# The new state of a recurrence made on VectorE ahead of the last tanh, instead of inside it

## The reference

```python
x = x + _L1_ffn_ref(_layernorm(x, axis=-1)[None], U_i, V_i, b_i, ...)[0]

def step(carry, xs):
    h, c = carry
    xi_t, xf_t, xg_t, xo_t = xs
    i_t = jax.nn.sigmoid(xi_t + h @ V_i)
    g_t = jnp.tanh(xg_t + h @ V_c)
    o_t = jax.nn.sigmoid(xo_t + h @ V_o)
    c_new = h * c + i_t * g_t
    h_new = o_t * jnp.tanh(c_new)
    return ((h_new, c_new), h_new)
```

## Time and profile before

| | |
|---|---|
| runs, us | 3303.53, 3307.72, 3311.19 |
| median, us | 3307.72 |
| span of the profiled execution, us | 3296.9 |
| TensorE busy with matmuls | 1510.9 us, 46% |
| VectorE busy | 1953.7 us, 59%, 13086 instructions |
| ScalarE busy | 1441.9 us, 44%, 8446 instructions |
| granted TensorE clock in the recurrence | 0.5 of full speed (1.2 GHz) |

### The profile page before, as it was taken

How to read it: one execution, slowest core, us unless ns; L and a number is a source line. 1 busy time by engine, 2 the same in 40 slices (tenths; PEclk the granted TensorE clock), 3 DMA queues, 4 the chain that set the end, 5 groups by cost and what they waited for, 6 DMA issues and landing times.

```text
span 3296.9 us, 86333 instructions
## 1 busy us (share of the span) xinstructions
PE 1510.9 (46%) x26414; PEld 1141.6 (35%) x26414; DVE 1953.7 (59%) x13086; ACT 1441.9 (44%) x8446; POOL 169.9 (5%) x130
## 2 busy tenths in 40 slices
PE   4989575434343434333443434343434343434343
PEld 4444323333333333333333333333333333333333
DVE  5557896555555555555555555555555555555555
ACT  5331134444444444444444444444444444444444
POOL 0620271000000000000000000000000000000000
PEclk8999885555555555555555555555555555555555
DMA  6010000000000000000000000000000000000000
GB/s 225 1 32 0 0 5 1 2 3 2 3 2 3 2 3 2 3 2 3 2 2 3 2 3 2 3 2 3 2 3 2 3 2 3 2 2 2 3 2 15
DMA packets 13012, 29.04 MB, mean 9 GB/s; under 512 B 1971, under 2 KB 9654, under 8 KB 10422
## 3 DMA queue, kind: packets, MB, share of 16 engines
q1 hardware_dynamic: 10406, 22.02, 1.9%
q10 hardware_dynamic: 2064, 0.55, 0.1%
HBM read 21.52 MB, written 1.05 MB: 7 GB/s over the span
## 4 chain that ended last, share of the span: by engine, by line
ACT 37%; PE 37%; DVE 15%; issue 9%; DMA 1%; SPq 0%; DVEq 0%; POOL 0%; ACTq 0%; POOLq 0%
PE psum L490 21%; ACT work L663 18%; ACT work L659 11%; DVE work L984 11%; ACT work L655 8%; PE psum L412 4%; PE psum L494 3%; PE psum L353 2%; PE psum L474 2%; PE psum L473 2%; PE psum L364 1%; DVE work L898 1%; DVE FT L935 1%; DMA work<-in_adj_dram 1%; PE psum L392 0%
## 5 line engine op out<-in xcount | busy, mean ns | idle before, releaser
L490 PE MATMUL psum<-work,MASK 128*128 128x1 f16 x18432 | 951.5, 168 | 1656.3 <-DVE work L984 1582.5
L490 PEld LDWEIGHTS psum<-work,MASK 128*128 128x128 bf16 x18432 | 802.7, 107 | 1817.5 <-DVE work L984 1741.0
L655 ACT ACTIVATE work<-psum 128x1 f32<-128x1 f32 x2048 | 351.2, 172 | 1471.0 <-PE psum L494 1471.0
L979 DVE TENSOR_SCALAR work<-work 128x1 f32<-128x1 f32 x2048 | 314.6, 154 | 732.1 <-ACT work L659 732.1
L663 ACT ACTIVATE work<-psum,work 128x1 f32<-128x1 f32 x2048 | 720.2, 352 | 0.0
L494 PE MATMUL psum<-work,MASK 128*128 128x1 f16 x6144 | 575.5, 168 | 0.0
L984 DVE CUSTOM_DVE_ANT_0 work<-work 128x1 f16<-128x1 f32 x2048 | 331.5, 162 | 295.3
L494 PEld LDWEIGHTS psum<-work,MASK 128*128 128x128 f16 x6144 | 432.3, 107 | 0.0
L990 DVE SCALAR_TENSOR_TENSOR work<-psum,work 128x1 f32<-128x1 f32 x2048 | 430.7, 210 | 0.0
L659 ACT ACTIVATE work<-psum 128x1 f32<-128x1 f32 x2048 | 414.9, 203 | 20.8 <-PE psum L494 20.8
L987 DVE TENSOR_TENSOR work<-work 128x1 f16<-128x1 f32 x2048 | 332.3, 162 | 72.1
(11 more groups left out here) (132 smaller groups left out, 1005.2 us busy)
## 6 DMA issues: line engine op xcount, KB each, us to landing
work<-in_adj_dram SPq DMA_DIRECT2D x16, 1024.0 KB, 5.3
work<-in_L_ffn_Wd_dram SPq DMA_DIRECT2D x4, 512.0 KB, 6.0
out_dram<-work SPq DMA_DIRECT2D x4, 256.0 KB, 2.4
work<-in_L_ffn_bd_dram SPq DMA_DIRECT2D x1, 512.0 KB, 6.8
W<-in_L_ffn_W_dram ACTq DMA_DIRECT2D x1, 256.0 KB, 2.8
watt<-in_L_gnn_w_att_dram ACTq DMA_DIRECT2D x2, 64.0 KB, 7.2
work<-in_L_gnn_Wq_dram SPq DMA_DIRECT2D x1, 64.0 KB, 8.1
Wfc<-in_L_gnn_W_fc_dram ACTq DMA_DIRECT2D x1, 64.0 KB, 5.8
```

The source lines that it names most:

```text
L490: nc.tensor.matmul(bank(NGATE * k + gate)[:, col:col + 1], Vparts[:, gate, part, :], h1[:, q:q + 1], start=False, stop=False, skip_group_c ...
L655: nc.scalar.activation(sig_i[:, q], bank(NGATE * k)[:, col:col + 1], ACT.Sigmoid).then_inc(i_ready, 1)
L979: v.tensor_scalar(o_scaled[:, q], sig_o[:, q], SCALE_H, None, ALU.mult).then_inc(o_scaled_ready, 1)
```

## The change

The tanh of g goes to a new SBUF column g_ in place of PSUM. VectorE waits for hc, sig_i and g at the head of its step and writes g * i + hc into PSUM bank 6 or 7. The last tanh waits for that alone (c_ready) and reads it, with no scale and no bias. Behind the product, VectorE does not make the state again; hc is made from the PSUM column, and the two waits there go.

```diff
-        c_, hc, tanh_c, sig_i, sig_o, o_scaled = (region(SMALL + 2 * k, 2) for k in range(6))
+        g_, hc, tanh_c, sig_i, sig_o, o_scaled = (region(SMALL + 2 * k, 2) for k in range(6))
...
-                    nc.scalar.activation(bank(6 + u % 2)[:, 0:1], bank(NGATE * k + 1)[:, col:col + 1], ACT.Tanh).then_inc(g_ready, 1)
+                    nc.scalar.activation(g_[:, q], bank(NGATE * k + 1)[:, col:col + 1], ACT.Tanh).then_inc(g_ready, 1)
...
-                    act.wait_ge(g_ready, t + 1)
-                    act.wait_ge(hc_ready, t + 1)
-                    nc.scalar.activation(tanh_c[:, q], bank(6 + u % 2)[:, 0:1], ACT.Tanh,
-                                         bias=hc[:, q], scale=sig_i[:, q]).then_inc(tanh_ready, 1)
+                    act.wait_ge(c_ready, t + 1)
+                    nc.scalar.activation(tanh_c[:, q], bank(6 + u % 2)[:, 0:1], ACT.Tanh).then_inc(tanh_ready, 1)
...
+                    dve.wait_ge(hc_ready, t + 1)
+                    dve.wait_ge(i_ready, t + 1)
+                    dve.wait_ge(g_ready, t + 1)
+                    v.scalar_tensor_tensor(bank(6 + u % 2)[:, 0:1], g_[:, q], sig_i[:, q], hc[:, q],
+                                           ALU.mult, ALU.add).then_inc(c_ready, 1)
                     dve.wait_ge(o_ready, t + 1)
                     v.tensor_scalar(o_scaled[:, q], sig_o[:, q], SCALE_H, None, ALU.mult).then_inc(o_scaled_ready, 1)
...
-                    dve.wait_ge(hc_ready, t + 1)
-                    v.scalar_tensor_tensor(c_[:, q], bank(6 + u % 2)[:, 0:1], sig_i[:, q], hc[:, q],
-                                           ALU.mult, ALU.add).then_inc(c_ready, 1)
-                    dve.wait_ge(c_ready, t + 1)
-                    v.scalar_tensor_tensor(hc[:, r], ring_h[:, u:u + 1], 1.0 / SCALE_H, c_[:, q],
+                    v.scalar_tensor_tensor(hc[:, r], ring_h[:, u:u + 1], 1.0 / SCALE_H, bank(6 + u % 2)[:, 0:1],
                                            ALU.mult, ALU.mult).then_inc(hc_ready, 1)
```

## The result

| | us |
|---|---|
| before, median (lowest to highest) | 3305.72 (3303.53 to 3311.19) |
| changed, median (lowest to highest) | 3669.31 (3666.64 to 3672.69) |
| ratio, 95% interval | 1.1101 (1.1085 to 1.1116) |
| span of the profiled execution, before and changed | 3296.9 and 3671.0 |

The change made the kernel 364 us slower. The forecast was 3577 with a range of 3480 to 3690; of the rivals, "the handoff or the write is dearer" stood at 3662 and 3686.

The account below looks back on a forecast made before the run. The prediction took the ring's latency per step as the bound: the path from the i gate to the product grows from 0.65 to 0.789 us, +0.139 in 1937 steps, 269 us, giving 3577 us; range 3480 to 3690.

Parts of the forecast that it names:

- the handoff or the write is dearer: Rival: g's handoff to VectorE takes 0.144 us (3662), or the state's PSUM write its upper bound (3686); chance 0.15.
- The path that sets the end: Latency once around the engines' ring of waits sets the time; TensorE's wait for the product grows some 265 us.
- The tie ahead of the product: Before, the tanh's path and the output gate's scaling path both reach VectorE's product at 0.65 us, within 0.01.
- The tanh at 0.172: ScalarE's last tanh, without its two operand columns, falls from 0.352 to 0.172 us, saving 0.180.
- The handoff from g to the state: From g's end on ScalarE to VectorE's state, behind a wait standing in front: 0.10 us.
- The state at 0.210: VectorE's new instruction making the state into PSUM lasts 0.210 us, like line 990 with the same operands.
- The handoff back and the last 0.03: From the state's end to ScalarE's tanh 0.035 us, and from the tanh's end to VectorE's product 0.03.
- How many steps pay: Of 2048 steps, 96 gate-input steps and 15 with TensorE stopped cover the added time; 1937 pay, 269 us.
- The scaling path at 0.02 under the tanh: VectorE's output gate scaling, now behind the state, lets the product start at 0.77 us, against 0.789 by the tanh.
- The rival that the wait in front costs no more than a carried one: Rival: g's handoff to the state takes 0.035 us instead of 0.10, giving 3451 us; chance 0.12.
- The missing overlap: Rival: VectorE's output gate scaling starts only after the state ends, adding 468 us, giving 3775; chance 0.05.
- Not slower: Rival: the tanh's saving pays for the detour, with handoff 0.035 and state 0.130 us, giving 3296; chance 0.03.

Follow-up runs that it names:

- 5: Kernel before with its last tanh plain, reading g alone without scale and bias operands: 3305.08 us, ratio 0.9981.
- 6: Kernel before with the output gate's factor given to the product instruction, dropping VectorE's separate scaling: 3302.73 us, ratio 0.9976.
- 7: Kernel before with both the plain last tanh of g alone and the output gate's factor in the product: 2963.43 us, ratio 0.8954.
- experiment 4: Changed kernel without VectorE's wait for i, so g stands alone on the wait in front of the state: 3619.16 us, ratio 1.0906.
- Experiment 8: Changed kernel with the state written to an SBUF column and read there by the last tanh: 3717.76 us, ratio 1.1234.
- Experiment 9: Changed kernel with g's wait carried by the state and the output gate's factor in the product, no separate scaling: 3470.16 us, ratio 1.0490.
- 1: Changed kernel with the state's three waits reordered to g, i, hc, so the state itself carries g's wait: 3465.89 us, ratio 1.0465.
- 2: Kernel before with the last tanh's two waits swapped, so hc's is carried and g's stands in front: 3418.21 us, ratio 1.0321.
- 3: Kernel before with the waits of VectorE's product swapped, so the tanh's stands in front: 3515.67 us, ratio 1.0623.
- 10: Kernel before, unchanged, timed against itself as a control: 3308.43 us, ratio 1.0001.
- 11: Kernel before with the output gate's factor in the product instruction, timed a second time beside the control: 3297.60 us, ratio 0.9971.

## Why the prediction was right, and what was mis-sized

The time lies in the range, but outside the 3545 to 3610 that the forecast gave itself: the range reached it because it also held the rival "dearer". By the prediction's own signs (the state lasts 0.21, 0.10 behind g) the forecast's sum was wrong in two terms, while the way round the ring, the tie and the direction were right.

- **The path that sets the end**: right. TensorE's wait for the product grew by 364 us, as the time did.
- **The tie ahead of the product**: right, shown by 5, 6 and 7. It is the reason why the tanh's 0.18 us could not have come back as a gain of that size even if the detour had been free.
- **The tanh at 0.172**: right, 0.171. Putting g into SBUF cost nothing: line 657 stays at 0.166, where I had added 0.006.
- **The handoff from g to the state, taken at 0.10 with bounds of 0.035 and 0.144**: this is the term that failed. It measured 0.144, the upper bound. I gave the row of line 858 more weight, since it goes from ScalarE to an ordinary instruction. That row was a wait with one semaphore, and the new one has two; experiment 4 shows 0.03 of the missing 0.044 to hang on that. The rest, some 0.015, lies between the wait and the instruction (0.060 against 0.043), and why stays open. That the rival's 0.144 was met is luck: it was read ahead of the custom product, where one semaphore (0.021) and a longer last piece (0.084) make it, not two semaphores (0.050) and 0.060.
- **The state at 0.210**: 0.227. Experiment 8 gives 0.008 of the 0.017 to the PSUM output. The other 0.009 is the state all in SBUF (0.219) over line 990 before (0.210), which read one column from PSUM; but line 990 also overlapped its forerunner, and the new state starts from idle. The scaling, the same instruction in both kernels, lasts 0.154 from idle and 0.149 overlapped, so about half of the 0.009 may be that. No run takes the two apart. The page of the Trainium skill that would have put 0.065 on the PSUM side (Perfetto Trace Analysis, Optimizing Scalar/DVE Operations) is not borne out on VectorE, where experiment 8 has 0.008; on ScalarE the same passage has SBUF dearer by 42 ns (93 against 51), and the 32 ns of experiment 8 point the same way.
- **The handoff back and the last 0.03**: right, 0.033 and 0.03.
- **Per step**: 0.139 forecast, 0.193 measured in the plain step. The two mis-sized terms make 0.044 + 0.017 = 0.061, less 0.006 for g.
- **How many steps pay**: 1937 forecast. The loop grew by 368.5 us, which is 1905 times 0.1934. The gate-input steps paid nothing: over a plain step they had 0.231 before and 0.038 after, so all of the 0.193 was covered, 18.5 us over 96 steps. The 30 longest steps, at the ends of the body, gave some 10 back (62.4 us over plain steps before, 52.2 after), which the forecast did not have.
- **The scaling path at 0.02 under the tanh**: right in kind, 0.04 in size. Line 982 starts at 0.51, and the product could have started at 0.51 + 0.149 + 0.144 = 0.80 against 0.84. Experiment 9 shows that it does not count. One sign that I had named was wrong: the product's idle time rose, from 295 to 368 us, where I had it fall. The scaling now begins inside the state, so it ends well ahead of the tanh (0.66 against 0.81), and the product idles behind it for longer.
- **The rival that the wait in front costs no more than a carried one** fell in 1, 2 and 3. The rival "dearer" is what happened in size, in both its terms, though not for the reason of its number. The missing overlap fell: line 982 starts 0.13 behind line 979's start, which lasts 0.227. "Not slower" fell with both of its terms, 0.144 where it had 0.035 and 0.227 where it had 0.130.

## What to carry to other kernels

In a loop of tiny instructions count the handoffs before the operations: a two-operand activation of 0.35 us was cheaper than a plain one of 0.17, because the VectorE instruction that replaced its operands brought 0.227 of its own and one more crossing each way. Where an instruction has several waits, write the one that comes last so that the instruction itself carries it; here three lines in another order were worth 203 of 364 us. And before taking time off one input of an instruction, look what else reaches it at the same moment: two inputs tied to 0.01 us, and shortening either alone brought at most 0.3%. A wait that has long been met is not free either where it shares the semaphore instruction in front with the one that comes last: leaving i's out brought 50 us. Of the kernels that compute the whole reference, the one before with the scale folded into the product is the fastest, by 0.3%.

## What the runs showed of the hardware that I had not expected

- The place of a wait is not free: behind a wait that stands in front of an instruction, with one semaphore, VectorE starts 0.117 (ordinary) to 0.141 us (custom) after the releaser's end, with two semaphores 0.145; carried by the instruction it is 0.03 (the product behind the tanh; 0.042 in experiment 1). On ScalarE 0.094 against 0.034. The semaphore instruction itself lasts 0.021 on VectorE with one semaphore, 0.050 with two, and 0.017 on ScalarE with one.
- VectorE's stops of some 0.25 us with nothing to wait for stand 128 of its instructions apart, or a multiple of that, those for semaphores and registers included (experiments 10 and 11). At some of the places of that row no stop shows.
- The output gate's sigmoid lasted 0.203 us behind a tanh that writes PSUM, and 0.180 behind the same tanh writing SBUF, itself 0.166 either way.
- A VectorE instruction with the same operands lasts 0.210 with one input column in PSUM (overlapping its forerunner), 0.219 with all columns in SBUF and 0.227 with inputs in SBUF and the output in PSUM (both from idle).
- The stops at the ends of the loop's body differ between kernels: 62.4 us over plain steps in the 30 longest before, 52.2 after. They do not go by the length of a step: it is 62.9 at 1.407 us in experiment 3 and 57.2 at 1.386 in experiment 1. The cause is open.
